# Adjacency counts of a graph network: order of the scalar engine's passes, of the first group, and banks of the transposes

## The reference

```
m = relu(x[src]) + EPS
z = m * t
zmax = segment_max(z, dst)
e = exp(z - zmax[dst])
denom = segment_sum(e, dst)
alpha = e / (denom[dst] + 1e-16)
agg = segment_sum(alpha * m, dst)
h = agg + x
h = relu(layernorm(h @ w1 + b1))
return h @ w2 + b2
```

## Time and profile before

| what | us |
|---|---|
| median of 3 runs | 991.01 |
| lowest, highest | 990.02, 991.46 |
| the profiled execution | 988.73 |
| its span, first to last instruction | 986.9 |
| PE busy | 900.9 (91%) |
| DVE busy | 698.4 (71%) |
| ACT busy | 501.1 (51%) |
| POOL busy | 380.4 (39%) |
| mean granted clock of PE | 0.976 |

### The profile page before, as it was taken

How to read it: one execution, slowest core, us unless ns; L and a number is a source line. 1 busy time by engine, 2 the same in 40 slices (tenths; PEclk the granted TensorE clock), 3 DMA queues, 4 the chain that set the end, 5 groups by cost and what they waited for, 6 DMA issues and landing times. The chain is left out here.

```text
span 986.9 us, 13353 instructions
## 1 busy us (share of the span) xinstructions
PE 900.9 (91%) x4281; PEld 680.1 (69%) x4281; DVE 698.4 (71%) x1286; ACT 501.1 (51%) x766; POOL 380.4 (39%) x326
## 2 busy tenths in 40 slices
PE   5998878789999999989999899799999999999980
PEld 3997555567887788868888687566666666666650
DVE  6856778867644766786667958588776666776665
ACT  2665467663543536343455124566566665556630
POOL 2003000035400652007511242677666667666540
PEclk9999999999999999999999979999999999999995
DMA  6433000033201221013200433499999999999868
GB/s 177 146 121 122 18 0 1 1 144 102 87 0 54 86 71 58 1 54 113 69 17 22 145 142 128 146 340 330 324 357 350 346 327 357 351 348 341 299 174 207
DMA packets 57163, 159.75 MB, mean 162 GB/s; under 512 B 13901, under 2 KB 21651, under 8 KB 48656
## 3 DMA queue, kind: packets, MB, share of 16 engines
q1 hardware_dynamic: 44725, 147.50, 43.4%
q0 software_dynamic: 12288, 11.36, 4.1%
q10 hardware_dynamic: 91, 0.13, 0.1%
HBM read 152.71 MB, written 25.58 MB: 181 GB/s over the span
## 5 line engine op out<-in xcount | busy, mean ns | idle before, releaser
L261 PE MATMUL ps<-split_operands 128*125 128x512 f32 (+5 forms) x690 | 266.7, 387 | 10.8 <-DVE split_operands L1340 4.6
L263 PE MATMUL ps<-split_operands 128*125 128x512 f32 (+5 forms) x690 | 260.7, 378 | 0.0
L262 PE MATMUL ps<-split_operands 128*125 128x512 f32 (+5 forms) x690 | 260.7, 378 | 0.0
L667 POOL DMA_INDIRECT yrow_scratch<-work,row_i x64 | 151.4, 2365 | 95.9 <-ACT work L1015 93.4
L261 PEld LDWEIGHTS ps<-split_operands 128*125 128x125 f32 (+3 forms) x690 | 130.0, 188 | 39.8 <-DVE split_operands L1340 5.2
L393 POOL TENSOR_TENSOR split_operands<-work,split_operands 128x512 fp32r<-128x512 f32 x66 | 83.5, 1293 | 167.9 <-ACT split_operands L375 153.8
L263 PEld LDWEIGHTS ps<-split_operands 128*125 128x125 f32 (+3 forms) x690 | 129.7, 188 | 26.6
L1563 DVE TENSOR_TENSOR gate_up_lo<-expert_weights,split_operands 128x2048 fp32r<-128x2048 f32 x64 | 146.4, 2288 | 0.5 <-ACT split_operands L997 0.5
L262 PEld LDWEIGHTS ps<-split_operands 128*125 128x125 f32 (+3 forms) x690 | 129.9, 188 | 23.8
L997 ACT ACTIVATE split_operands<-expert_weights 128x2048 fp32r<-128x2048 f32 x64 | 121.8, 1903 | 0.0
L2065 PE MATMUL ps<-expert_weights,work 128*117 128x512 f32 x256 | 120.3, 592 | 0.5 <-issue 0.5
(11 more groups left out here) (222 smaller groups left out, 1326.7 us busy)
## 6 DMA issues: line engine op xcount, KB each, us to landing
expert_weights<-experts_in SPq DMA_DIRECT2D x64, 1024.0 KB
expert_weights<-experts_in SPq DMA_DIRECT2D x64, 512.0 KB, 9.1
work<-w_in SPq DMA_DIRECT2D x12, 1024.0 KB, 5.1
yrow_scratch<-work SPq DMA_DIRECT2D x5, 1500.0 KB
split_operands<-yrow_scratch SPq DMA_DIRECT2D x4, 1120.0 KB
work<-cw_in SPq DMA_DIRECT2D x3, 1024.0 KB, 5.2
work<-rows_in SPq DMA_DIRECT2D x10, 256.0 KB, 4.7
work<-wmix_in SPq DMA_DIRECT2D x4, 512.0 KB, 5.2
```

The lines of the kernel that those rows point to most:

```text
L261: pe.matmul(o, a[1], b[0], start=start, stop=False)
L262: pe.matmul(o, a[0], b[1], start=False, stop=False)
L263: return pe.matmul(o, a[0], b[0], start=False, stop=stop)
L667: pool.indirect_dma_start(yrow, bass.IndirectOffsetOnAxis(ap=row_i[:, e:e + 1], axis=0), OS[e % 4], None, bounds_check=last_row, oob_is_er ...
```

## The change

Three things change in the code, and nothing in what is computed.

1. ACT's Abs pass stands ahead of the wait for the slot. It waits for the Relu before it (`last_one_hot`), which is the reader of `apart`; the Relu now waits for the slot.
2. DVE makes the one-hots of the first group ahead of `mix_add(NT - 1)`. For this it waits for `x_rows` (POOL's additions, whose operands lie where the one-hots go), and the first use of the slots is allowed by DVE itself, at the program's start.
3. The transposes of odd tiles go to banks 6 and 7 and those of even tiles to 4 and 5, and they wait for the low parts of the tile before the last.

```diff
             def adj_to_hi(j):
                 act.wait_ge(S("adj_tr"), j + 1)
-                act.activation(AT_hi[:, 0:3, cut(j * T, T)], ps[0:T, 4, 0:3 * T].rearrange("p (s n) -> p s n", s=3), ACT.Copy)
+                act.activation(AT_hi[:, 0:3, cut(j * T, T)], ps[0:T, 4 + 2 * (j % 2), 0:3 * T].rearrange("p (s n) -> p s n", s=3), ACT.Copy)
...
-            def last_of_group(group, lo):
-
+            def last_of_group(group, lo, first=False):
+
+                if not first:
+                    act.wait_ge(S("last_one_hot"), group)
+                act.activation(apart, iota_h, ACT.Abs, scale=-1.0, bias=srcf[:, bass.ds(lo + G - 1, 1)]).then_inc(S("apart"), 1)
                 act.wait_ge(S("one_hot_free"), group * G + G)
-                act.activation(apart, iota_h, ACT.Abs, scale=-1.0, bias=srcf[:, bass.ds(lo + G - 1, 1)]).then_inc(S("apart"), 1)
                 act.wait_ge(S("apart"), group + 1)
                 act.activation(one_hot_src[:, G - 1, :], apart, ACT.Relu, scale=-1.0, bias=one_c[:]).then_inc(S("last_one_hot"), 1)
...
-                last_of_group(before, lo)
+                last_of_group(before, lo, not j)
...
+            dve.sem_inc(S("one_hot_free"), G)
...
-            mix_add(NT - 1)
...
+            dve.wait_ge(S("x_rows"), NT)
             for j in range(NT):
...
                 one_hots(before, lo, near)
+                if not j:
+                    mix_add(NT - 1)
                 with dve.Fori(1, groups + 1) as q:
...
                 pe.wait_ge(S("adj_sb"), j + 1)
-                if j >= 1:
-                    pe.wait_ge(S("adj_lo"), j)
+                if j >= 2:
+                    pe.wait_ge(S("adj_lo"), j - 1)
                 for s in range(NT):
-                    b, q = (4, s) if s < 3 else (5, s - 3)
+                    b, q = 4 + 2 * (j % 2) + s // 3, s % 3
...
-                if not j:
-                    last.then_inc(S("one_hot_free"), G)
```

More of the change, by code:

```diff
@@ L843, in adj_to_hi @@
                 act.wait_ge(S("adj_tr"), j + 1)
-                act.activation(AT_hi[:, 0:3, cut(j * T, T)], ps[0:T, 4, 0:3 * T].rearrange("p (s n) -> p s n", s=3), ACT.Copy)
-                act.activation(AT_hi[:, 3:5, cut(j * T, T)], ps[0:T, 5, 0:2 * T].rearrange("p (s n) -> p s n", s=2),
+                act.activation(AT_hi[:, 0:3, cut(j * T, T)], ps[0:T, 4 + 2 * (j % 2), 0:3 * T].rearrange("p (s n) -> p s n", s=3), ACT.Copy)
+                act.activation(AT_hi[:, 3:5, cut(j * T, T)], ps[0:T, 5 + 2 * (j % 2), 0:2 * T].rearrange("p (s n) -> p s n", s=2),
                                ACT.Copy).then_inc(S("adj_hi"), 1)
@@ L1279, in _ @@
                     tile_ranges()
-            mix_add(NT - 1)
             def adj_low(j):
                 dve.wait_ge(S("adj_hi"), j + 1)
-                dve.tensor_tensor(AT_lo[:, 0:3, cut(j * T, T)], ps[0:T, 4, 0:3 * T].rearrange("p (s n) -> p s n", s=3),
+                dve.tensor_tensor(AT_lo[:, 0:3, cut(j * T, T)], ps[0:T, 4 + 2 * (j % 2), 0:3 * T].rearrange("p (s n) -> p s n", s=3),
                                   f(AT_hi[:, 0:3, cut(j * T, T)]), ALU.subtract)
-                dve.tensor_tensor(AT_lo[:, 3:5, cut(j * T, T)], ps[0:T, 5, 0:2 * T].rearrange("p (s n) -> p s n", s=2),
+                dve.tensor_tensor(AT_lo[:, 3:5, cut(j * T, T)], ps[0:T, 5 + 2 * (j % 2), 0:2 * T].rearrange("p (s n) -> p s n", s=2),
                                   f(AT_hi[:, 3:5, cut(j * T, T)]), ALU.subtract).then_inc(S("adj_lo"), 1)
```

## The result

| | before | after |
|---|---|---|
| median, us | 990.51 (4 runs) | 977.91 (4 runs) |
| lowest, highest | 984.86, 991.46 | 976.86, 978.50 |
| profiled execution, us | 988.73 | 976.86 |
| its span | 986.9 | 975.0 |
| PE busy in the span | 900.9 (91%) | 908.5 (93%) |

The ratio is 0.9883, with a 95% interval of 0.9845 to 0.9922. The forecast was 981.9 with a range from 979.5 to 987.0. The direction and the main mechanism were right. By the interval the gain is between 7.7 and 15.4 us; the two profiled executions differ by 11.9. The forecast was counted from a median of 991.01; from the 990.51 of this table it would be 981.4.

What follows compares the result with a forecast made beforehand. Hand-overs between PE, ACT and DVE, not one engine's work, were taken to bound the adjacency-count stage. Gains of 5.8 + 2.15 + 1.15 = 9.1 us gave 981.9 us, own range 979.5 to 984, with rival 1 to 987.

Steps and rivals of the forecast that it cites:

- The Abs pass leaves the ring: Adjacency-count stage: Abs no longer waits for PE, ACT needs 1.92 us a group, DVE's pace holds; gain 5.8 us.
- The 29 steps: DVE's group-to-group steps inside tiles, from group 1 to the last: 64.67 us before, forecast 58.86 with DVE unhindered.
- I leave the four as they are: The four DVE group steps that cross from one tile to the next, 16.97 us together, were forecast unchanged.
- The first group: Start of the stage: first one-hots move ahead of the last residual addition, near 110.83; group 1 starts earlier, gain 2.15 us.
- The banks: Transposes in four PSUM banks wait for the low parts of tile j-2; forecast worth nothing, between 0 and 0.15 us.
- The tail: From the last group's start to aggregation: PE's last pair comes earlier, then DVE is late next; gain 1.15 us.
- The clock: PE's dip to 1.2 GHz from 205.7 to 208.9, costing 1.3 us, was left in place; the range allows its vanishing.
- Rival 1: In the stage, hand-overs keep part of the gain: each of 29 steps loses about 0.15, 4.4 us, 986.3; chance 0.12.
- Rival 2: PE falls to its lower clock inside the stage: 30 us more than forecast if throughout, 1012; chance 0.03.
- Rival 3: The clock dip after the stage grows over the first two destination tiles: 7.2 us more, 989.1; chance 0.03.
- Rival 4: Abs still starts behind PE's release, something else holding ACT; only the front's 2.15 us is left, 988.9; chance 0.02.

Runs made afterwards that it cites:

- e7_held: The changed kernel, with DVE held ahead of each next tile's register loads until PE has read the last slot of the tile before; 984.72 us in one execution.

## Why the prediction was wrong in size

**The Abs pass leaves the ring: right.** Its hand-over from the Relu was put at 0.25 us, between 0.03 and 0.27. Measured are 0.2 (5.6 us in 26 waits). ACT therefore doesn't bind, and DVE sets the pace at 1.98 to 2.03 us a group. The 29 steps took 58.41 us where 58.86 were summed. The 0.45 less comes from taking one step of 2.04 for tiles 1 to 4; the steps measured are 1.98 to 2.03, but for the first of tile 4, which took 2.28 (2.24 before).

**"I leave the four as they are": the step that failed.** The sum took the crossings over unchanged, on the ground that the loads have to run in any case. They do, but when they may start was set by a wait of the last one-hot, which the change lets go earlier. The prediction asked when PE frees the slot for the next tile's first one-hot, and not what held the loads ahead of it. A term put at nothing measured 2.06 us, and the range had no room for it: without it the time would have been 980.0, inside the range. The rows that told it were in the trace of before: the load at 129.1, 0.98 us behind the one-hots, while at the start of the stage the first load begins with the addition ahead of it (both at 111.9; 1.71 us from that addition's start to the first one-hot).

**The first group: right.** 2.10 for 2.15, and the first one-hot came at 110.92 for 110.83. **The banks: right** at nothing (0.07). **The tail: right**, 1.24 for 1.15. DVE comes to the low parts of tile 3 at 4.57 us behind the last group's start (186.82 to 191.39), where 4.67 was forecast, and it is late next, as the last row of the long listing above shows: PE waits for L1301.

**The clock: wrong in the likeliest case, and left open in the range.** The dip after aggregation's start was left, with 1.3 us for its vanishing in the range. It vanished, and was worth 1.56. The ground for leaving it was an idle gap of about the same length. The gap is about the same (PE is busy 1.15 of the last 3 us, and was 1.05), and yet the dip is gone; what PE does in the groups ahead may count too, which isn't shown. Up to aggregation, 9.1 + 2.06 + 0.5 (steps, start and tail) are 11.7 us. The 1.56 was then given back in the profiled execution, mostly in the router part; that the medians ended at 12.6 and not at 11.9 isn't a success of any term. The range ended at 979.5 since it held the clock's term but not the crossings'.

**Rivals.** Rival 1 (hand-overs keep part) didn't come: of the 29 steps only that of 2.28 lost its 0.15. Rival 2 (PE's clock falls in the stage) didn't come with the change, but e7_held shows that it exists, with longer pauses of PE. With the change's four banks and PE's short pauses the granted clock stayed at 1.00 from 113 to 190 us. Rival 3 didn't come, rather the reverse. Rival 4 is refuted by the waits.

## What to carry to other kernels

When a wait is the bound, ask what the engine's sequencer could have done while it was held: register loads behind the wait start earlier too, and the gain can be larger than the wait. When a buffer is filled in two passes, the wait for the buffer belongs in front of the second. And where PE pauses at the end of a stage, look at the granted clock of the next one, in more than one trace, before a difference of 1 us is put down to an edit.

## What the runs showed of the hardware

Register loads on DVE took about 0.7 us each (from the second of three at 129.1 to the first one-hot at 130.53 stand two). They are hidden only by what the sequencer is ahead, and with them moved in among one-hot pairs of 0.46 us the stage was no shorter (9.52 us of crossings rather than 14.91, but the stretch 73.15 rather than 73.32).

Pauses of PE of 1.31 to 1.70 us at three crossings in e7_held brought the granted clock down to the 1.2 GHz level (0.50 from 149 to 151 us) inside a stage that held 2.4 GHz in the kernels before and after. A pause of 1.22 us, at the first crossing, didn't, nor did the 0.66 us in each group of the kernel before, nor one of 2.09 us at the start of its stage. So the length of a single pause doesn't decide. Eight matmuls of zeros, which made PE busy 2.78 rather than 1.05 of the last 3 us ahead of aggregation, kept the clock at 1.00 behind it in two of two executions.
